# Recurrent stage of a two-layer decoder: the input added to the output projection by a product with the unit matrix, the sum copied by ScalarE

## The chip, the core and the metric

The kernel runs on one core of a Trainium2 chip. The core has five engines that each work through a queue of their own: TensorE (PE, matrix products; its results go to the accumulator memory PSUM), VectorE (DVE), ScalarE (ACT), GpSimd (POOL) and SyncE (SP, which here only starts transfers). They wait for one another through semaphores. The metric is the device time of one execution of the whole kernel in microseconds (us). Durations of single instructions are given in us too, unless marked ns. TensorE's clock has two levels, 1.2 and 2.4 GHz; the profile gives the granted clock as a share of the upper one, so that 0.50 is 1.2 GHz for a whole stretch and 1.00 is 2.4 GHz.

## The reference, cut to what matters

The whole is a decoder of two layers over x of (8, 256, 128). The change is in the second layer's recurrent ("mamba") part, four blocks in a row, each of which adds its result to its input:

```python
def _mamba(x, in_w, cw, cb, xw, dtw, dtb, A_log, Dp, ow):
    xz = x @ in_w
    u, z = jnp.split(xz, 2, axis=-1)
    ...
    u = jax.nn.silu(conv)
    dbl = u @ xw
    dt = jax.nn.softplus(dbl[..., :DT_RANK] @ dtw + dtb)
    ...
    y = _selective_scan(u, dt, A, Bm, Cm, Dp)
    y = y * jax.nn.silu(z)
    return y @ ow

def _forward(x, ...):
    for i in range(N_BLOCKS):
        h = _layer_norm(x, norm_w[i], norm_b[i])
        h = _mamba(h, in_proj_w[i], ...)
        x = x + h
    return _layer_norm(x, fn_w, fn_b)
```

The line `x = x + h` is what the change moves to other engines. The scan inside is `h = dA_t * h + dBu_t` over time, for 256 channels and 16 states each.

## The kernel before, in words

The stages of the decoder follow one another: opening (linear attention), cross attention, feed-forward, a norm, the recurrent stage (`mamba_stage`, from about 480 to 1399 us of the span), a norm, cross attention, experts, store. The change touches `mamba_stage` alone.

In this stage the tokens lie along the free axis, 2048 in all, in four quarters of 512 columns. The stage works on units that this text calls **frames**: frame f is block f // 4 and quarter f % 4, so there are 16 of them (NF). The running x of the residual lies in `xm` (the same buffer as `c.xn`, 128 channels by 2048 columns), one slice `cols(f)` per quarter, which frame f + 4 reads again.

Within a frame 16 **items** (t = 0 to 15, k = 16 f + t) go through a pipeline over four engines:

- GpSimd `times_b(k)` (L1586) makes the input of the scan, 128x1024, into one of 8 slots of `hs`, three items ahead of the scan;
- ScalarE `decay(k)` (L1769, two instructions of 512 columns) writes the decay factors into one of two pairs of PSUM banks. It may do so only when the item two before is done with them, so it runs one item ahead of VectorE and waits for VectorE's work on item k - 2;
- VectorE `scan(k)` (L1905) runs the recurrence over 1024 columns. For 11 items of 16 it multiplies the outcome by C as well (`times_c`, L1911); for t = 0, 4, 6, 10, 14 GpSimd does that (L1594);
- TensorE `sum_y` (L1663) adds up the states of four items in PSUM.

Between the items stand, at fixed values of t, the steps of the frames before and behind. On VectorE: `gate(f - 1, 1)` at t = 1, `step_size(f + 1)` at t = 8 (L1888), `gate(f, 0)` at t = 9 (L1894), `residual(f - 1)` at t = 11 (L1899) and `scaled_x(f + 2)` at t = 14 (L1880). On ScalarE: `silus(f + 1)` at t = 2 (L1797 to L1804, two loads of the function table and four activations, which need the projections of TensorE), `square` at t = 10, `inv_std` at t = 13, `affine` at t = 15 (L1793, it writes `hn`, the normalized input of the next frame), and four copies `kv_copy` (L1777) at t = 4, 7, 12, 14.

TensorE's order is written out by hand too. The part that matters is this: at the start of a frame `tap_projection(F, 0)` (L1630, four products of 512 columns; it waits for `hn`), `sum_y` of the last four items of the frame before, `skip`, `tap_projection(F, 1)`, `gate_projection`, `x_projection`; later in the frame `centre(G)` (L1690), `out_projection(f - 1)` (L1671), one `kv_job`, `average(G)` (L1694), another `kv_job`, `sum_y(f, 2)`. `average(G)` overwrites the PSUM bank PA that `out_projection(f - 1)` has filled, so it waits for the semaphore `resid`, which the residual raises. A product of fp32 operands is two MATMUL instructions in the trace; so `out_projection`, two products, is x4 there, and a tap projection is x8.

The residual of frame f - 1 is read again by `centre(f + 3)`, one frame and more later, and by the norm behind the stage; the transfers of the weights of blocks 2 and 3 wait for `resid` as well.

After the last frame come `gate(15, 1)`, `out_projection(15)` and `residual(15)`, and then all engines meet before the norm.

`w.prepare` and `rates` are GpSimd's and ScalarE's work on the next block's weights in frames 2, 6 and 10; these three are called prepare frames here.

Of the kernel before, what the change touches and what calls it, by code (L numbers as in the profile page):

```python
# [12 lines left out]
ALU = mybir.AluOpType  # L13
ACT = mybir.ActivationFunctionType
# [1374 lines left out]
def mamba_stage(c, g):  # L1389
# [31 lines left out]
    with Stage(c, "ma") as s:  # L1421
# [89 lines left out]
        with nc.Block() as block:  # L1511
# [109 lines left out]
            def _(pe):  # L1621
# [45 lines left out]
                def out_projection(f):  # L1667
                    b = (f // QUARTERS) % 2
                    pe.wait_ge(gated, 2 * f + 2)
                    for h in range(2):  # L1670
                        mm = pe.matmul(c.ps[:, PA, :], w_out[:, b, h, :], z[:, f % 3, h, :], start=(h == 0), stop=(h == 1))  # L1671
                    mm.then_inc(out_ps, 1)

# [81 lines left out]
            def _(act):  # L1755
# [50 lines left out]
                def x_rows(F):  # L1806
# [3 lines left out]
                    act.activation(xp[0:XB, :], c.ps[0:XB, PB, :], ACT.Copy).then_inc(xp_done, 1)  # L1810

                def magnitude(F):
                    if F >= 1:
                        act.wait_ge(dt_out0, 32 * F)
                        act.wait_ge(dt_out1, 32 * F)
                    for h, bank in ((0, PA), (1, PB)):
                        act.wait_ge(dt_ps, 2 * F + h + 1)
                        a = act.activation(dtu[:, h, :], c.ps[:, bank, :], ACT.Abs)
                    a.then_inc(abs_done, 1)
# [27 lines left out]
                for f in range(NF):  # L1847
                    F, G = f + 1, f + 2
                    for t in range(ITEMS):
# [16 lines left out]
                        if G < NF:  # L1866
                            if t == 10:
                                square(G)
                            if t == 13:
                                inv_std(G)  # L1870
                            if t == 15:
                                affine(G)
                        if t == 14 and f % QUARTERS == 1 and f // QUARTERS + 1 < NBLK:
                            rates(f // QUARTERS + 1)

            @block.vector
            def _(dve):
# [17 lines left out]

                def residual(f):
                    dve.wait_ge(out_ps, f + 1)
                    x = xm[:, cols(f)]
                    dve.tensor_tensor(x, x, c.ps[:, PA, :], ALU.add).then_inc(resid, 1)  # L1899

                def scan(k):
# [15 lines left out]
                for f in range(NF + 1):  # L1917
                    F, G = f + 1, f + 2
                    if f == NF:
                        gate(f - 1, 1)  # L1920
                        residual(f - 1)
                        break
                    for t in range(ITEMS):
# [8 lines left out]
                        if t == 9:  # L1932
                            gate(f, 0)
                        if t == 11 and f >= 1:
                            residual(f - 1)
                        if t == 14 and G < NF:
# [305 lines left out]
```

## Time and profile before

| | us |
|---|---|
| median of 3 runs | 1829.61 |
| lowest, highest | 1823.79, 1832.76 |
| the profiled execution, its own time | 1830.69 |
| span of the profiled execution, first to last instruction | 1829.0 |
| VectorE busy in the span | 1443.8 (79%) |
| TensorE busy | 1330.1 (73%) |
| GpSimd busy | 1141.3 (62%) |
| ScalarE busy | 1106.2 (60%) |
| mean granted TensorE clock | 0.851 |

The shares are means over stages with different limits. What bears on this change is the recurrent stage alone. A frame is measured below from one `scaled_x` (L1880) on VectorE to the next; fourteen of these lie in the loop, from 571.96 to 1283.60 us.

### The profile page before, as it was taken

The page shows a single profiled execution, that of the slowest core. Times are in us where ns is not written, and L with a number is a line of the kernel's source. Part 1 is how long each engine was busy: PE and PEld are TensorE (multiplying, and loading weights), DVE is VectorE, ACT ScalarE, POOL GpSimd, SP SyncE. Part 2 cuts the span into 40 slices and gives each one's busy share as a digit, 9 for nine tenths or more (in the row PEclk, how much of TensorE's full clock was granted, in tenths as well). Part 3 has the DMA queues.
Part 4 walks back from the last instruction along what each step waited for, and adds up shares of the span by engine and source line. Part 5 has one row for each costly group of instructions (what it writes and reads, how often), then busy time and mean ns, then how long its engine had stood idle before and what let it go on. Part 6 is the DMA issues. An engine that isn't in the chain of part 4 may idle for free. (4 is left out here: it accounts for less than half of the span.)

```text
span 1829.0 us, 23410 instructions
## 1 busy us (share of the span) xinstructions
PE 1330.1 (73%) x6866; PEld 650.4 (36%) x6867; DVE 1443.8 (79%) x2463; ACT 1106.2 (60%) x2434; POOL 1141.3 (62%) x742
## 2 busy tenths in 40 slices
PE   6777998966757557767557657557645798899878
PEld 4554555643222112222112222112201555565523
DVE  4664888877259999999999999999996577777634
ACT  4444887856565566665566665566643677677630
POOL 2111665640079999999999999999993244444400
PEclk9998999995678777787777878778867799999979
DMA  3000000000054443353454343444224111211000
GB/s 98 1 2 1 2 2 1 1 25 1 6 221 152 184 185 145 122 192 128 184 191 160 133 161 132 186 185 173 106 103 137 48 47 50 91 46 47 1 0 23
DMA packets 70218, 168.04 MB, mean 92 GB/s; under 512 B 20420, under 2 KB 40152, under 8 KB 56664
## 3 DMA queue, kind: packets, MB, share of 16 engines
q1 hardware_dynamic: 68680, 166.17, 24.5%
q8 instruction: 49, 0.80, 0.2%
q10 hardware_dynamic: 1168, 0.53, 0.1%
q14 instruction: 65, 0.53, 0.1%
q0 software_dynamic: 256, 0.01, 0.0%
HBM read 131.03 MB, written 35.65 MB: 91 GB/s over the span
## 5 line engine op out<-in xcount | busy, mean ns | idle before, releaser
L1586 POOL TENSOR_TENSOR ma_hs<-ma_dtuR,ma_Bt 128x1024 f32<-128x1024 f32 x256 | 597.0, 2360 | 30.4 <-PE ps L1663 23.3
L1769 ACT ACTIVATE ps<-ma_dtR,ma_A 128x512 f32<-128x512 f32 x512 | 332.6, 682 | 314.3 <-DVE ma_hs L1911 271.5
L844 POOL TENSOR_TENSOR x_pr<-x_pr,x_rec 128x512 f32<-128x512 f32 x256 | 267.7, 1046 | 293.1 <-DVE x_rec L1084 293.1
L1905 DVE TENSOR_TENSOR_SCAN ps<-ps,ma_hs 128x1024 f32<-128x1024 f32 x176 | 401.8, 2283 | 1.9 <-POOL ma_hs L1586 1.8
L1050 ACT ACTIVATE x_pr<-x_sm,x_mx 128x256 f32<-128x256 f32 x512 | 255.3, 500 | 71.6 <-DVE x_mx L1075 68.9
L1663 PE MATMUL ps<-ma_hs,ma_fold 128*32 128x512 f32 x1024 | 163.9, 770 | 163.2 <-POOL ma_hs L1594 151.0
L1911 DVE TENSOR_TENSOR ma_hs<-ps,ma_Ct 128x1024 f32<-128x1024 f32 x176 | 215.4, 1224 | 6.1
L1905 DVE TENSOR_TENSOR_SCAN ma_hs<-ps,ma_hs 128x1024 f32<-128x1024 f32 x80 | 182.5, 2281 | 31.0 <-ACT ps L1769 28.7
L1630 PE MATMUL ps<-ma_hn,ma_w_tap 128*128 128x512 f32 (+3 forms) x256 | 145.1, 721 | 79.0 <-ACT ma_hn L1793 79.0
L1594 POOL TENSOR_TENSOR ma_hs<-ma_hs,ma_Ct 128x1024 f32<-128x1024 f32 x80 | 188.5, 2356 | 13.5 <-DVE ma_hs L1905 13.5
L906 PE MATMUL ps<-ident,x_pr 128*128 128x128 f32 x1024 | 163.2, 286 | 5.8 <-DVE x_pT L984 4.6
L906 PEld LDWEIGHTS ps<-ident,x_pr 128*128 128x128 f32 x1024 | 113.9, 143 | 76.4 <-issue 50.3
L1663 PEld LDWEIGHTS ps<-ma_hs,ma_fold 128*32 128x32 f32 x1024 | 33.3, 131 | 282.6 <-issue 157.9
L1075 DVE CUSTOM_DVE_ANT_0 x_sm<-x_sm,x_neg 128x256 f32<-128x256 f32 x256 | 110.1, 466 | 26.3 <-DVE x_sm L1071 26.3
L1071 DVE TENSOR_TENSOR x_sm<-ps,x_m 128x512 f32<-128x512 f32 x128 | 86.8, 678 | 46.9 <-PE ps L896 45.9
L1630 PEld LDWEIGHTS ps<-ma_hn,ma_w_tap 128*128 128x128 f32 x256 | 58.6, 236 | 166.4 <-issue 166.4
L1075 DVE CUSTOM_DVE_ANT_0 x_sm<-ps,x_mr 128x256 f32<-128x256 f32 x256 | 97.5, 418 | 22.9 <-PE ps L896 19.9
L896 PE MATMUL ps<-x_k,x_q 64*128 64x256 f32 x512 | 74.5, 410 | 30.5 <-DVE x_sm L1071 29.8
L1050 ACT ACTIVATION_READ_ACCUMULATOR x_pr<-x_sm,x_mx 128x1 f32 x512 | 96.4, 188 | 0.0
L984 DVE COPY x_pT<-ps 128x512 f32<-128x512 f32 x128 | 86.5, 676 | 4.8 <-PE ps L906 4.5
L986 ACT ACTIVATE x_pT<-ps 128x512 f32<-128x512 f32 x128 | 74.5, 583 | 21.6 <-PE ps L906 21.2
L659 DVE TENSOR_TENSOR la_sc<-ps,la_tri 128x512 f32<-128x512 f32 x64 | 43.3, 680 | 48.2 <-PE ps L442 48.2
(307 smaller groups left out, 2222.6 us busy)
## 6 DMA issues: line engine op xcount, KB each, us to landing
ma_dtuR<-ma_dtu_d SPq DMA_DIRECT2D x32, 1024.0 KB, 6.8
ma_dtR<-ma_dt_d SPq DMA_DIRECT2D x32, 1024.0 KB, 8.9
ma_Bt<-ma_bc_d SPq DMA_DIRECT2D x16, 1024.0 KB, 4.9
ma_Ct<-ma_bc_d SPq DMA_DIRECT2D x16, 1024.0 KB, 7.4
ma_dtu_d<-ma_dtu SPq DMA_DIRECT2D x32, 256.0 KB, 2.0
ma_dt_d<-ma_dt SPq DMA_DIRECT2D x32, 256.0 KB, 2.3
keys_d<-ma_kv SPq DMA_DIRECT2D x32, 256.0 KB, 5.0
values_d<-ma_kv SPq DMA_DIRECT2D x32, 256.0 KB, 2.6
```

Of the source, the lines that this page charges most:

```text
L844: pool.tensor_tensor(pr[:, r, :, :], pr[:, r, :, :], rec[:, r, :].unsqueeze(2).broadcast_to([P, 2, L]), ALU.mult).then_inc(pr_done, 1)
L906: mm = pe.transpose(c.ps[:, 2 + n % 2, kt * L + t * P:kt * L + (t + 1) * P], pr[:, n % RP, t, kt * P:(kt + 1) * P], c.ident[:, :])
L1050: a = act.activation(pr[:, n % RP, t, :], sm[:, n % 2, t, :], ACT.Exp, bias=mx[:, n % 2, t:t + 1], scale=-1.0, accum_out=den[:, n % RP, t: ...
L1071: dve.tensor_tensor(sm[:, n % 2, :, :], bank, m[:, ds(b * 2, 2), :], ALU.mult).then_inc(s_free, 1)
L1075: a = dve.tensor_tensor_reduce(sm[:, n % 2, t, :], bank[:, t, :] if small else sm[:, n % 2, t, :], mr[:, p, :] if small else neg[:, t, :], ...
L1586: pool.tensor_tensor(hs[:, k % SLOTS, :, :], dtuR[:, unit(f, h), q, :].unsqueeze(1).broadcast_to([P, 2, CH]), rows(Bt, k), ALU.mult).then_ ...
L1594: pool.tensor_tensor(hs[:, k % SLOTS, :, :], hs[:, k % SLOTS, :, :], rows(Ct, k), ALU.mult).then_inc(c_pool, 1)
L1630: mm = pe.matmul(out, w_tap[:, b, TAPS - 1 - e, h * P:(h + 1) * P], src, start=(e == 0), stop=(e == TAPS - 1), skip_group_check=True)
L1663: mm = pe.matmul(c.ps[q * E32:(q + 1) * E32, Y[h], :], fold[:, :], hs[:, (k0 + q) % SLOTS, a, :], start=False, stop=(j % 2 == 1 and a == 1 ...
L1769: e = act.activation(c.ps[:, 2 * (k % 2) + a, :], dtR[:, unit(f, h), q, :], ACT.Exp, scale=A[:, (f // QUARTERS) % 2, h, q, no:no + 1])
L1905: dve.tensor_tensor_scan(out, pair(k), slot(k), 0.0, ALU.mult, ALU.add).then_inc(scan_done, 1)
L1911: dve.tensor_tensor(hs[:, k % SLOTS, :, :], c.ps[:, 2 * (k % 2):2 * (k % 2) + 2, :], rows(Ct, k), ALU.mult).then_inc(c_vector, 1)
```

## The change

It takes the addition of `residual` off VectorE. TensorE adds a third product to the accumulation group of `out_projection`: the unit matrix `c.ident` times the slice of `xm`, so that the bank PA holds x + h. ScalarE copies the bank to `xm` at t = 11, in front of the `kv_copy` of t = 12, and raises `resid`; the last of them stands behind ScalarE's loop.

```diff
                     for h in range(2):
-                        mm = pe.matmul(c.ps[:, PA, :], w_out[:, b, h, :], z[:, f % 3, h, :], start=(h == 0), stop=(h == 1))
-                    mm.then_inc(out_ps, 1)
+                        pe.matmul(c.ps[:, PA, :], w_out[:, b, h, :], z[:, f % 3, h, :], start=(h == 0), stop=False)
+                    pe.matmul(c.ps[:, PA, :], c.ident[:, :], xm[:, cols(f)], start=False, stop=True).then_inc(out_ps, 1)
...
+                def residual(f):
+                    act.wait_ge(out_ps, f + 1)
+                    act.activation(xm[:, cols(f)], c.ps[:, PA, :], ACT.Copy).then_inc(resid, 1)
...
+                        if t == 11 and f >= 1:
+                            residual(f - 1)
...
+                residual(NF - 1)
...
-                def residual(f):
-                    dve.wait_ge(out_ps, f + 1)
-                    x = xm[:, cols(f)]
-                    dve.tensor_tensor(x, x, c.ps[:, PA, :], ALU.add).then_inc(resid, 1)
...
-                        residual(f - 1)
...
-                        if t == 11 and f >= 1:
-                            residual(f - 1)
```

On VectorE, items 9 to 12 of frame 1 stand in this order before. L1894 is the gate, L1905 a scan, L1911 its product with C, L1899 the residual:

```order
L1894 TENSOR_TENSOR ma_z<-ps,ma_z 128x512
L1905 SCALAR_TENSOR_TENSOR ma_hs<-ps,ma_hs 128x1024
L1905 SCALAR_TENSOR_TENSOR ps<-ps,ma_hs 128x1024
L1911 TENSOR_TENSOR ma_hs<-ps,ma_Ct 128x1024
L1899 TENSOR_TENSOR xn<-xn,ps 128x512
L1905 SCALAR_TENSOR_TENSOR ps<-ps,ma_hs 128x1024
```

The same place in the changed kernel, whose lines lie three to eight further down (L1902 gate, L1908 scan, L1914 product with C):

```order
L1902 TENSOR_TENSOR ma_z<-ps,ma_z 128x512
L1908 SCALAR_TENSOR_TENSOR ma_hs<-ps,ma_hs 128x1024
L1908 SCALAR_TENSOR_TENSOR ps<-ps,ma_hs 128x1024
L1914 TENSOR_TENSOR ma_hs<-ps,ma_Ct 128x1024
L1908 SCALAR_TENSOR_TENSOR ps<-ps,ma_hs 128x1024
```

The scan of item 12 follows directly on the product of item 11.

On ScalarE, items 8 to 13 of frame 1 before (L1781 is `square`, L1769 `decay`, L1777 `kv_copy`, L1785 and L1787 `inv_std`):

```order
L1769 ACTIVATE ps<-ma_dtR,ma_A 128x512 x6
L1781 ACTIVATE ma_sq<-ps 128x512
L1769 ACTIVATE ps<-ma_dtR,ma_A 128x512 x4
L1777 ACTIVATE ma_kv<-ps 128x512
L1769 ACTIVATE ps<-ma_dtR,ma_A 128x512 x2
L1785 ACTIVATE ma_rstd<-ps,eps 128x512
```

and now:

```order
L1769 ACTIVATE ps<-ma_dtR,ma_A 128x512 x6
L1781 ACTIVATE ma_sq<-ps 128x512
L1769 ACTIVATE ps<-ma_dtR,ma_A 128x512 x2
L1814 ACTIVATE xn<-ps 128x512
L1769 ACTIVATE ps<-ma_dtR,ma_A 128x512 x2
L1777 ACTIVATE ma_kv<-ps 128x512
L1769 ACTIVATE ps<-ma_dtR,ma_A 128x512 x2
L1785 ACTIVATE ma_rstd<-ps,eps 128x512
```

The new copy (L1814) stands between the decays of items 12 and 13; everything else keeps its place. On TensorE the piece from `skip` to the second `kv_job` of a frame is now

```order
L1655 MATMUL ps<-ma_u,ma_dD 128x512
L1690 MATMUL ps<-xn,centre 128x512
L1671 MATMUL ps<-ma_z,ma_w_out 128x512 x2
L1672 MATMUL ps<-xn,ident 128x512
L1680 MATMUL ps<-cT,ma_w_kv 128x512
L1694 MATMUL ps<-ma_sq,average 128x512
L1680 MATMUL ps<-cT,ma_w_kv 128x512
```

with L1672 as the only row that was not there before.

## Rows read from the trace of the kernel before

**Rows 1.** Waits of VectorE, 560 to 1450 us: waiting <- waited for: us, times, longest.

```profile
DVE ma_hs L1905 <- ACT ps L1769: 21.0, 12, 1.9
...
DVE ma_z L1894 <- PE ps L1663: 5.3, 6, 3.4
```

**Rows 2.** Stretches: us, busy PE, PEld, DVE, ACT, POOL (instructions), PEclk, DMA share, GB/s.

```profile
737.48:792.09 54.61, 36.28 (x112) 12.19 (x112) 52.38 (x34) 33.90 (x51) 51.28 (x26) 0.78 0.43 160
...
846.69:901.81 55.12, 34.94 (x112) 11.73 (x112) 52.74 (x35) 33.87 (x51) 54.84 (x31) 0.79 0.39 143
901.81:956.17 54.36, 35.11 (x112) 11.79 (x112) 52.30 (x35) 33.90 (x51) 53.10 (x27) 0.81 0.43 168
```

**Rows 3.** VectorE in order of time: start us, us, instruction, [idle before <- releaser].

```profile
946.45 0.68 DVE L1899 TENSOR_TENSOR xn<-xn,ps 128x512 f32<-128x512 f32 x1
947.04 2.29 DVE L1905 TENSOR_TENSOR_SCAN ps<-ps,ma_hs 128x1024 f32<-128x1024 f32 x1
```

**Rows 4.** TensorE in order of time: three first tap projections and one second.

```profile
574.33 6.30 PE L1630 MATMUL ps<-ma_hn,ma_w_tap 128*128 128x512 f32 x8 [4.31 <-ACT ma_hn L1793]
...
739.87 5.46 PE L1630 MATMUL ps<-ma_hn,ma_w_tap 128*128 128x512 f32 x8 [5.24 <-ACT ma_hn L1793]
...
904.17 5.22 PE L1630 MATMUL ps<-ma_hn,ma_w_tap 128*128 128x512 f32 x8 [5.50 <-ACT ma_hn L1793]
...
912.14 3.58 PE L1630 MATMUL ps<-ma_hn,ma_w_tap 128*128 128x512 f32 x8
```

**Rows 5.** VectorE's waits in the frames of these three taps.

```profile
582.55 0.69 DVE L1894 TENSOR_TENSOR ma_z<-ps,ma_z 128x512 f32<-128x512 f32 x1 [0.81 <-PE ps L1663]
...
592.01 2.29 DVE L1905 TENSOR_TENSOR_SCAN ma_hs<-ps,ma_hs 128x1024 f32<-128x1024 f32 x1 [1.85 <-ACT ps L1769]
...
756.71 2.29 DVE L1905 TENSOR_TENSOR_SCAN ma_hs<-ps,ma_hs 128x1024 f32<-128x1024 f32 x1 [1.85 <-ACT ps L1769]
...
920.78 2.29 DVE L1905 TENSOR_TENSOR_SCAN ma_hs<-ps,ma_hs 128x1024 f32<-128x1024 f32 x1 [1.68 <-ACT ps L1769]
```

**Rows 6.** Stretches in which the granted clock rises, columns as in Rows 2.

```profile
579.00:580.00 1.00, 1.00 (x2) 0.29 (x2) 1.00 (x1) 0.62 (x2) 1.00 (x2) 0.67 0.15 4
...
743.00:744.00 1.00, 1.00 (x3) 0.36 (x2) 1.00 (x2) 0.16 (x1) 1.00 (x1) 0.75 0.00 0
...
907.00:908.00 1.00, 1.00 (x4) 0.43 (x3) 1.00 (x1) 0.27 (x1) 1.00 (x2) 0.83 0.00 0
...
1289.00:1290.00 1.00, 1.00 (x3) 0.26 (x2) 1.00 (x2) 0.10 (x2) 1.00 (x1) 0.68 0.00 0
```

**Rows 7.** ScalarE around the place of the copy, a prepare frame and a plain one.

```profile
888.78 1.29 ACT L1769 ACTIVATE ps<-ma_dtR,ma_A 128x512 f32<-128x512 f32 x2
892.20 1.30 ACT L1769 ACTIVATE ps<-ma_dtR,ma_A 128x512 f32<-128x512 f32 x2 [2.13 <-DVE ma_hs L1911]
...
943.12 1.30 ACT L1769 ACTIVATE ps<-ma_dtR,ma_A 128x512 f32<-128x512 f32 x2 [0.98 <-DVE ma_hs L1905]
946.56 1.30 ACT L1769 ACTIVATE ps<-ma_dtR,ma_A 128x512 f32<-128x512 f32 x2 [2.15 <-DVE ma_hs L1911]
947.80 0.57 ACT L1777 ACTIVATE ma_kv<-ps 128x512 f32<-128x512 f32 x1
```

**Rows 8.** TensorE in the same two places.

```profile
888.08 1.88 PE L1671 MATMUL ps<-ma_z,ma_w_out 128*128 128x512 f32 x4
889.80 1.02 PE L1680 MATMUL ps<-cT,ma_w_kv 128*128 128x512 f32 x2
...
941.06 1.02 PE L1680 MATMUL ps<-cT,ma_w_kv 128*128 128x512 f32 x2
947.18 2.08 PE L1694 MATMUL ps<-ma_sq,average 128*128 128x512 f32 x2 [5.09 <-DVE xn L1899]
```

**Rows 9.** The end of the stage, VectorE and TensorE.

```profile
1398.81 0.69 DVE L1899 TENSOR_TENSOR xn<-xn,ps 128x512 f32<-128x512 f32 x1 [2.14 <-PE ps L1671]
...
1396.82 1.96 PE L1671 MATMUL ps<-ma_z,ma_w_out 128*128 128x512 f32 x4 [0.91 <-DVE ma_z L1894]
```

More of the change, by code:

```diff
@@ L1868, in _ @@
                                 square(G)
+                        if t == 11 and f >= 1:
+                            residual(f - 1)
+                        if G < NF:
                             if t == 13:
```

## The prediction

> **What bounds the kernel now.** I read the page's shares first and then left them, since the change touches one stage only. In the recurrent stage I cut VectorE's order of time into frames, from one `scaled_x` to the next, and asked for busy time in each [rows 2]. The reader is to see that VectorE is busy 52.30 to 52.74 of 54.36 to 55.12 us in a frame, GpSimd 51.28 to 54.84 (next to nothing left in a prepare frame, 3 us in a plain one), ScalarE 33.9 and TensorE 35 to 36. So VectorE sets the pace and GpSimd is 3 us behind it. Next VectorE's waits [rows 1]: what it waits for in the stage is above all ScalarE's `decay`, 21.0 us in 12 waits, and TensorE's `sum_y` ahead of a gate, 5.3 us. The 12 waits lie at one place of the frame, ahead of the scan of item 4, some 19 us behind `scaled_x` [rows 5].
>
> Where they come from is seen in TensorE's rows [rows 4]. The chain is `scaled_x`, `affine`, first tap projection, `sum_y` and `skip`, second tap projection, gate and x projections, `silus`, then `decay`, then the scan. The second tap projection takes 3.58 us, the first 5.22, 5.46 and 6.30 us: the same work, but it starts behind an idle time of 4.3 to 5.5 us with a granted clock of 0.50 (1.2 GHz), and the clock goes to 1.00 (2.4 GHz) while it runs. From the granted clock of one microsecond each [rows 6] the rise can be placed: 0.67 over 579 to 580 puts it at 579.66, 0.75 at 743.50, 0.83 at 907.34, 0.68 over 1289 to 1290 at 1289.64. For the three frames with rows:
>
> - tap starts 574.33, rise 5.33 later, tap takes 6.30, VectorE then loses 0.81 + 1.85 = 2.66;
> - tap starts 739.87, rise 3.63 later, 5.46, loses 1.85;
> - tap starts 904.17, rise 3.17 later, 5.22, loses 1.68 [rows 4 to 6].
>
> So tap length is 3.58 plus half the time up to the rise, and VectorE's loss in the frame is the excess over 3.58, nearly to the hundredth. One more thing stands in these rows: the rises are 163.84, 163.84 and 382.30 us apart, which is 3, 3 and 7 times 54.61, although the frames between them took 54.36, 54.61 and 55.12 [rows 2]. The rises don't follow the taps. It is the frame that settles at them: 737.48 to 792.09 is 54.61 long.
>
> **The change part by part.**
>
> *VectorE.* Residual removed, 16 times. It costs 0.68 us by itself, but 947.04 - 946.45 = 0.59 from start to start [rows 3]. Fifteen lie in the loop and are on the path: 15 x 0.59 = 8.9 us. The one at the end is below. Without it a plain frame is 54.36 - 1.68 - 0.59 = 52.09 us of VectorE plus the loss at item 4.
>
> *What is late next.* The chain to item 4 starts at `scaled_x` on VectorE. If VectorE is there 0.59 earlier, the tap starts 0.59 earlier too, but its clock rises where it did, so the tap ends only half as much earlier: the loss grows by 0.3 us. In the next frame the tap would be earlier by another 0.59 + what is left, and so on, until the frame is again as long as the distance of the rises. That is at 52.09 + loss = 54.61, loss 2.52. By the three pairs above, loss is 1.68 + 0.45 for each us beyond 3.17, so 2.52 belongs to a tap that starts 5.0 us ahead of the rise. That lies inside what the trace shows, 5.33 us at 574.33 with a loss of 2.66. I therefore expect the frames to come back to 54.6 us, with everything in the frame 5.0 - 3.6 = 1.4 us earlier against the rises, once and not per frame. Of the 8.9 us nearly all is given back: earlier by 1.4 at the last first-tap; then the last such loss is larger by 2.52 - 1.85 = 0.7; then two residuals (items 11 of the last two frames, the last of which has no tap) save 1.18. Net 1.9 us at the end of the loop.
>
> A rule stands against this. The Trainium skill, page "TensorE: Matmul & The Clock Gate", section "Part 1: The HAM clock gate (the "warmup" mystery)", says that for modeling the ramp penalty is small against a kernel and advises not to fit to it; by that rule the clock would be left out and the sum would be the full 8.9 us less the tail. The same section says that the clock's activity monitor is free-running and does not reset with the kernel; the even spacing in [rows 6] agrees with that.
>
> *GpSimd.* It has nothing new. In prepare frames it sets part of the pace; the third stretch of VectorE's wait there is GpSimd's [rows 2]. VectorE may be 0.59 earlier at item 12 against a `times_b` that is behind in those three frames; bounds 0 and 0.6 us each, I take 0, since the longer wait at item 4 hands GpSimd 0.7 us there.
>
> *ScalarE.* One copy of 128x512 from PSUM, 0.57 us as `kv_copy` takes [rows 7], 15 times in the loop. ScalarE would be idle: between the decays of items 12 and 13 it waits 2.15 us for VectorE in the plain frame, 2.13 in the prepare frame. Cost nothing if `out_ps` is there. Behind the copy on its queue stands `decay` of item 13, and for that VectorE's scan 13.
>
> *TensorE.* The product with the unit matrix: two products back to back take 889.80 - 888.08 = 1.72, so 0.86 each at 2.4 GHz and twice that at 1.2 [rows 8]. In the plain frame `out_projection` ends at 941.1 to 941.2; the sum is there at 942.0, and ScalarE reaches the copy at 944.4, 2.4 us later. In the prepare frame it ends at 889.9, sum at 890.8, copy done by 891.4; `decay` of item 13 starts at 892.20. Margin 0.8 us. So 0 in both, with an upper bound under the rivals. `average`, which now waits 5.09 us for VectorE's residual [rows 8], gets its bank about 2 us sooner; its outcome is read at t = 13 by ScalarE, which is not waiting for it, so nothing is gained.
>
> *The tail.* Here all is serial [rows 9]: the product lies ahead of the copy, + 0.86, and a copy of 0.57 stands for an addition of 0.69, - 0.12. Together + 0.75 us (0.6 to 1.6, the upper end at 1.2 GHz).
>
> *Sum* against the profiled execution: 1829.0 - 1.9 + 0.75 = 1827.85 us of span. The execution's own time lies 1.7 above its span and 1.1 above the median; taken off the median of 1829.61, the change of -1.15 gives 1828.5 us.
>
> **The rivals.**
>
> *A: the clock takes nothing back.* The loss at item 4 stays 1.7 to 1.85 (the rise moves with the tap, or the idle time ahead of it is no longer long enough). Then 8.9 - 0.75 = 8.1 us are gained: 1821.5. For it: a low clock needs some cause, and VectorE's path is otherwise clean. Against it: four rises at multiples of 54.61 [rows 6], and a tap that still follows an idle time of about 5 us [rows 4].
>
> *B: ScalarE's copy comes late.* Place: the three prepare frames, where GpSimd makes `sum_y` and so `out_projection` late. It decides once the sum is there more than 0.8 us later than worked out above. If the whole group runs at 1.2 GHz, three products are later by 0.86 each, 2.6 us, and `decay` of item 13 by 1.8, three times: 5.4 us. In plain frames the same leaves 942.0 + 2.6 = 944.6, copy done 945.2 before 946.56, no loss. Time up to 1829.6 - 1.15 + 5.4 = 1833.9, slower than before. For it: moving 1.4 us against the rises does bring more of this group under the low clock. Against it: the margin, and that a late frame pays less at its tap.
>
> *C: the low clock lasts through the whole tap.* It would then take 2 x 3.58 = 7.16 and cost VectorE 3.58 in each of some 13 frames, 1.73 more than 1.85, against 0.59 saved: + 1.14 x 13 = 15 us, 1844. It decides where the rise comes more than 5.33 us behind the tap's start, longer than any in the rows, and the rises would have to leave their spacing.
>
> **How the numbers follow.** The clock gives back the saving (1828.5): 0.66. A: 0.17. B: 0.10. C: 0.07. The range takes in A and the upper end of B and leaves out C and the outer half of A's spread: 1821 to 1834, which is also about where the runs of before lie (1823.79 to 1832.76), and these show that a median of a few runs moves by some us. A measurement of this kernel can tell about 0.5%, 9.1 us, from no change. A lies at 0.44% and is over that bound in less than half of its cases: 0.07, with 0.03 from the rest 0.10 for faster. C and a little of B: 0.08 slower. Within 0.5%: 0.82.
>
> **What would show it.** Right: VectorE's busy time in a plain frame 51.7 instead of 52.3, the frame still 54.6; the first taps 6.0 to 6.1 us long, starting 5 us ahead of the rise; VectorE's waits in the stage larger by 0.6 to 0.7 us per frame, a part of them ahead of `gate(f - 1, 1)` at t = 1. A shows as taps of 5.2 to 5.5 and frames of 54.0. B as ScalarE waiting for TensorE ahead of the copy and VectorE for `decay` at item 13. C as taps of 7.16. My number falls if the frame's length is neither 54.6 nor 54.0, or if the first taps become shorter than 5.

## The result

The changed kernel takes 1823.08 us in the median of 22 runs (1819.43 to 1830.06), the kernel before 1830.70 in 22 runs beside it (1823.79 to 1833.92). The ratio is 0.9967, with a 95% interval of 0.9956 to 0.9977: 4 to 8 us less, about a third of a percent. Ten of the 22 runs of the changed kernel lie between 1825.1 and 1830.1 us, at mean granted clocks of 0.854 to 0.858, where runs of the kernel before lie too; the other twelve, the profiled execution of 1821.99 us among them, lie between 1819.4 and 1823.1, at 0.859 to 0.863. The profiled execution has a span of 1820.3 us, against 1829.0 before.

The page of the changed kernel, busy time of the engines:

```profile
span 1820.3 us, 23474 instructions
...
PE 1331.4 (73%) x6898; PEld 647.3 (36%) x6899; DVE 1435.7 (79%) x2447; ACT 1114.2 (61%) x2450; POOL 1140.7 (63%) x742
```

VectorE's 1443.8 us have become 1435.7. Whether that is where the 8.7 us of span went is another question, and by the frames it is not. These are stretches of the changed kernel as in [rows 2], a frame each, and then the whole from the first `scaled_x` in the loop to the norm behind the stage (columns: us, busy PE, PEld, DVE, ACT, POOL with instructions, PEclk, DMA share, GB/s):

```profile
736.77:791.28 54.51, 36.71 (x114) 11.96 (x114) 51.79 (x33) 34.41 (x52) 50.99 (x26) 0.81 0.44 160
1009.77:1064.31 54.54, 36.74 (x114) 11.98 (x114) 51.80 (x34) 34.53 (x53) 51.26 (x26) 0.81 0.49 176
...
572.24:1401.15 828.91, 540.44 (x1697) 177.08 (x1697) 780.36 (x481) 504.48 (x767) 782.69 (x390) 0.80 0.40 150
```

The last of these in the kernel before:

```profile
571.96:1399.81 827.85, 527.30 (x1664) 173.91 (x1665) 789.19 (x497) 495.99 (x751) 782.85 (x390) 0.79 0.40 150
```

VectorE is busy 0.6 us less in each frame (51.79 against 52.38 in [rows 2]), and the frame is nearly as long as it was, 54.51 against 54.61. Only the first three frames of the loop are shorter by more than 0.1 us (54.85, 55.30 and 54.39 against 55.43, 55.51 and 54.58). Over the whole stretch VectorE has 8.8 us less to do and the stretch is 1.1 us longer. The recurrent stage gained nothing in this pair of executions.

The first tap projections of the changed kernel, to be read beside [rows 4]:

```profile
793.64 6.02 PE L1630 MATMUL ps<-ma_hn,ma_w_tap 128*128 128x512 f32 x8 [4.59 <-ACT ma_hn L1793]
...
848.20 6.05 PE L1630 MATMUL ps<-ma_hn,ma_w_tap 128*128 128x512 f32 x8 [4.56 <-ACT ma_hn L1793]
```

the wait that has grown on VectorE, beside [rows 5]:

```profile
801.58 0.69 DVE L1902 TENSOR_TENSOR ma_z<-ps,ma_z 128x512 f32<-128x512 f32 x1 [0.53 <-PE ps L1663]
...
811.05 2.29 DVE L1908 TENSOR_TENSOR_SCAN ma_hs<-ps,ma_hs 128x1024 f32<-128x1024 f32 x1 [1.85 <-ACT ps L1769]
```

and the rises of the clock, beside [rows 6]:

```profile
798.00:799.00 1.00, 1.00 (x3) 0.53 (x2) 1.00 (x1) 0.94 (x2) 1.00 (x2) 0.79 0.15 4
907.00:908.00 1.00, 1.00 (x3) 0.40 (x2) 1.00 (x2) 0.67 (x2) 1.00 (x2) 0.68 0.00 0
1289.00:1290.00 1.00, 1.00 (x2) 0.34 (x1) 1.00 (x2) 0.89 (x2) 1.00 (x2) 0.53 0.00 0
```

The rises are at 798.42, 907.64 and 1289.94, that is 109.22 and 382.30 apart, 2 and 7 times 54.61, as before. The tap at 793.64 starts 4.8 us ahead of its rise (3.7 before, for the tap at 794.45), takes 6.02 us (5.47), and VectorE loses 0.53 + 1.85 = 2.38 us (1.85). What the residual had cost, VectorE now spends waiting.

So in this pair the gain lies behind the stage. There the two kernels run the same instructions. The first stretch goes from the first product of the norm to the first of the router (the products with which the expert stage starts), the second from there to the end; before and after in turn:

```profile
1399.81:1747.93 348.12, 300.26 (x1841) 192.48 (x1841) 238.59 (x836) 245.56 (x711) 136.91 (x132) 0.95 0.17 60
...
1747.93:1828.90 80.97, 65.07 (x172) 23.55 (x172) 33.79 (x34) 5.50 (x10) 2.18 (x2) 0.79 0.05 13
```

```profile
1401.15:1743.26 342.11, 293.47 (x1841) 188.14 (x1841) 239.35 (x836) 245.09 (x711) 136.74 (x132) 0.98 0.17 61
...
1743.26:1820.30 77.04, 59.72 (x172) 21.56 (x172) 33.51 (x34) 5.49 (x10) 2.19 (x2) 0.84 0.05 14
```

TensorE is busy 6.8 us less with the same 1841 instructions, at a granted clock of 0.98 instead of 0.95, and the stretch is 6.0 us shorter; then 5.3 us less with the same 172, at 0.84 instead of 0.79, and 3.9 us shorter. 9.9 us in all, less 1.1 that the recurrent stage took longer and 0.3 that the changed execution was behind at the first `scaled_x` of the loop: 8.6, the 8.7 us of span but for rounding.

Last, the new operations. In a prepare frame, beside [rows 7]:

```profile
888.80 1.29 ACT L1769 ACTIVATE ps<-ma_dtR,ma_A 128x512 f32<-128x512 f32 x2
890.88 0.60 ACT L1814 ACTIVATE xn<-ps 128x512 f32<-128x512 f32 x1 [0.79 <-PE ps L1672]
891.97 1.30 ACT L1769 ACTIVATE ps<-ma_dtR,ma_A 128x512 f32<-128x512 f32 x2 [0.48 <-DVE ma_hs L1914]
```

ScalarE reaches the copy 0.79 us too early, and 0.48 us are still left ahead of the decay of item 13. At the end of the stage, beside [rows 9]:

```profile
1395.66 3.69 PE L1671 MATMUL ps<-ma_z,ma_w_out 128*128 128x512 f32 x4 [0.91 <-DVE ma_z L1902]
1399.19 1.02 PE L1672 MATMUL ps<-xn,ident 128*128 128x512 f32 x2
```

`out_projection` runs at the lower clock here nearly to its end, 3.69 us instead of 1.96.

### The profile page after: what moved, and what is told of

Read it like the earlier page. It is cut to its first block and busy times, and to the rows that moved or that the text cites. A ratio compares the mean times of both kernels' runs of the same rounds, so it can differ in the third digit from the quotient of the medians.

```text
span 1820.3 us, 23474 instructions
## 1 busy us (share of the span) xinstructions
PE 1331.4 (73%) x6898; PEld 647.3 (36%) x6899; DVE 1435.7 (79%) x2447; ACT 1114.2 (61%) x2450; POOL 1140.7 (63%) x742
## 5 line engine op out<-in xcount | busy, mean ns | idle before, releaser
L1769 ACT ACTIVATE ps<-ma_dtR,ma_A 128x512 f32<-128x512 f32 x512 | 332.7, 682 | 294.6 <-DVE ma_hs L1914 251.7
L1908 DVE TENSOR_TENSOR_SCAN ps<-ps,ma_hs 128x1024 f32<-128x1024 f32 x176 | 401.8, 2283 | 2.1 <-POOL ma_hs L1586 2.0
L1914 DVE TENSOR_TENSOR ma_hs<-ps,ma_Ct 128x1024 f32<-128x1024 f32 x176 | 215.5, 1224 | 6.0
L1908 DVE TENSOR_TENSOR_SCAN ma_hs<-ps,ma_hs 128x1024 f32<-128x1024 f32 x80 | 182.5, 2281 | 31.3 <-ACT ps L1769 28.0
L1630 PE MATMUL ps<-ma_hn,ma_w_tap 128*128 128x512 f32 (+3 forms) x256 | 152.2, 751 | 72.8 <-ACT ma_hn L1793 72.8
L1075 DVE CUSTOM_DVE_ANT_0 x_sm<-x_sm,x_neg 128x256 f32<-128x256 f32 x256 | 110.8, 468 | 24.9 <-DVE x_sm L1071 24.9
L1075 DVE CUSTOM_DVE_ANT_0 x_sm<-ps,x_mr 128x256 f32<-128x256 f32 x256 | 97.7, 420 | 22.7 <-PE ps L896 16.9
```

The lines of the kernel that those rows point to most:

```text
L1075: a = dve.tensor_tensor_reduce(sm[:, n % 2, t, :], bank[:, t, :] if small else sm[:, n % 2, t, :], mr[:, p, :] if small else neg[:, t, :], ...
L1630: mm = pe.matmul(out, w_tap[:, b, TAPS - 1 - e, h * P:(h + 1) * P], src, start=(e == 0), stop=(e == TAPS - 1), skip_group_check=True)
L1769: e = act.activation(c.ps[:, 2 * (k % 2) + a, :], dtR[:, unit(f, h), q, :], ACT.Exp, scale=A[:, (f // QUARTERS) % 2, h, q, no:no + 1])
L1908: dve.tensor_tensor_scan(out, pair(k), slot(k), 0.0, ALU.mult, ALU.add).then_inc(scan_done, 1)
L1914: dve.tensor_tensor(hs[:, k % SLOTS, :, :], c.ps[:, 2 * (k % 2):2 * (k % 2) + 2, :], rows(Ct, k), ALU.mult).then_inc(c_vector, 1)
```

## The experiments

Two theories on the frames: **G**, VectorE's saving is given back because the first tap starts earlier against a rise of the clock that doesn't move with it; and its rival, that the loss at item 4 is ScalarE's own or has some other cause. On the gain behind the stage there were three in turn: **E** (the expert stage meets less low clock), **L** (it depends on where the norm starts against the rises), **P** (it is the one product more at the end of the stage).

### Filling products ahead of the first tap, in both kernels

```diff
                     if F < NF:
+                        if F >= 2:
+                            pe.wait_ge(lnv_done, F + 1)
+                            for _n in range(5):
+                                pe.matmul(c.ps[:, PA, :], c.ident[:, :], c.cT[:, 0:CH], start=True, stop=True)
                         tap_projection(F, 0, PA)
```

> The kernel before, with five products more on TensorE (unit matrix times a constant tile, into bank PA, results unused) between the last sum of a frame and the first tap projection, in frames 2 to 15: they fill 4.3 of the 5.2 to 5.5 us in which TensorE waits there. Theory G (the clock gives back): with the clock at its upper level the first tap takes 3.6 to 4 us, VectorE's loss at item 4 falls from 1.85 to about 0 and frames are 52.7 to 53 us; 14 frames, 20 to 26 us less, 1805 to 1811. If the loss is ScalarE's own (its two table loads and four activations, whatever the clock): taps shorter, loss unchanged, 1829 to 1831.

> The changed kernel with the same filling products. Theory G: with no low clock at the tap nothing gives the residual's 0.59 us back, so VectorE alone would allow frames of 52.1 us, 8 us less than the kernel before with the filling. GpSimd's own work is 51.25 us in a plain frame and 54.8 to 55 in a prepare frame, 52.6 on the mean of four, so it may hold the frames there: then 1 to 4 us less than the kernel before with the filling, and waits of VectorE for GpSimd. If the residual is given back for another reason: the same time as the kernel before with the filling.

Measured: 1818.39 us from before (ratio 0.9938, 0.9920 to 0.9956) and 1807.15 from the changed kernel (0.9881, 0.9860 to 0.9902). A tap, VectorE's wait at item 4 and a plain frame, of the filled kernel before:

```profile
1004.56 3.65 PE L1630 MATMUL ps<-ma_hn,ma_w_tap 128*128 128x512 f32 x8 [0.85 <-ACT ma_hn L1797]
...
1019.84 2.29 DVE L1909 TENSOR_TENSOR_SCAN ma_hs<-ps,ma_hs 128x1024 f32<-128x1024 f32 x1 [0.34 <-ACT ps L1773]
...
1002.20:1055.22 53.02, 37.98 (x122) 12.42 (x120) 52.30 (x34) 33.79 (x52) 50.45 (x25) 0.84 0.51 181
1055.22:1110.95 55.73, 38.80 (x125) 13.07 (x124) 52.70 (x35) 33.76 (x51) 55.45 (x32) 0.85 0.38 142
```

and the frames of the filled changed kernel, with the stretch from the first `scaled_x` to the norm:

```profile
1000.37:1052.79 52.42, 38.71 (x122) 12.80 (x121) 51.70 (x33) 34.33 (x53) 50.28 (x26) 0.84 0.52 183
1052.79:1108.55 55.76, 39.32 (x126) 13.28 (x125) 52.10 (x33) 34.87 (x52) 55.48 (x32) 0.85 0.36 137
...
572.63:1381.29 808.66, 571.59 (x1833) 190.57 (x1832) 779.23 (x481) 503.52 (x767) 783.32 (x390) 0.85 0.41 154
```

The tap takes 3.65 us, VectorE's loss is 0.34: it was the clock. ScalarE's table loads and activations are all still there, so the rival falls. And now the change delivers: plain frames of 52.42 against 53.02, 0.60 us, where the forecast had 0.59 for the residual. The second prepare frame and the third are 55.7 in both, with GpSimd busy 55.5 of it. Of the thirteen frames in the loop eight are 0.5 to 0.7 shorter and five are not: two prepare frames, two frames behind a prepare frame in which VectorE waits 1.04 and 1.10 us for GpSimd, and one of 54.28 us, 1.2 longer than in the filled kernel before. That one is the clock again. The filling products themselves started at the lower clock (its rise is at 894.9) and took 5.73 us, where a filling of nine instructions at the upper clock took 4.03, and VectorE waits 1.85 us for `decay` at item 4; from the filled changed kernel:

```profile
892.52 5.73 PE L1705 MATMUL ps<-cT,ident 128*128 128x512 f32 x10
898.08 3.58 PE L1630 MATMUL ps<-ma_hn,ma_w_tap 128*128 128x512 f32 x8
```

The stretch is 808.66 against 814.05, 5.4 us. I had expected 20 to 26 us from the filling alone and got 12, in part because two prepare frames got longer by 0.5 and 0.6 (55.12 before) instead of shorter. The 11.2 us between the two medians are more than either branch expected. In the profiles 5.4 of them are this stage's; the stretch from the norm to the router is 349.2 against 347.8, and the one behind it 81.0 against 75.1, although the edit touches neither.

### The same saving with the other sign

Each frame's addition done twice:

```diff
                         if t == 11 and f >= 1:
+                            dve.wait_ge(out_ps, f)
+                            dve.tensor_tensor(spare[:, :], xm[:, cols(f - 1)], c.ps[:, PA, :], ALU.add)
                             residual(f - 1)
```

> The kernel before with the residual's addition done twice in each frame, once into an unused tile: 0.59 us more for VectorE in 15 frames, the change's saving with the other sign. Theory G: the frames stay at 54.4 to 54.6 us, VectorE's loss at item 4 falls from 1.85 to about 1.3, first taps start 1.2 us nearer to the rise and take 4.9; the loop from the third scaled_x to the last stays at 711 to 713 us. If VectorE's work counts in full: frames 55.1 to 55.2, loop 718, kernel 9 us slower, 1839. What the later stages make of it I can't say, up to 6 us either way.

Measured: 1841.95 us (1.0068, 1.0053 to 1.0084), frames of 55.0 to 56.4, and a loop of 722.6 us from the third `scaled_x` to the last instead of the 711 to 713 expected (711.6 before). Theory G as I had put it is too broad: an addition is not swallowed. Two taps that follow one another:

```profile
853.83 5.11 PE L1631 MATMUL ps<-ma_hn,ma_w_tap 128*128 128x512 f32 x8 [5.58 <-ACT ma_hn L1794]
...
909.21 6.42 PE L1631 MATMUL ps<-ma_hn,ma_w_tap 128*128 128x512 f32 x8 [5.90 <-ACT ma_hn L1794]
```

With longer frames the taps slide towards the rise: the one at 853.83 starts 2.9 us ahead of it and takes 5.11. The next doesn't take 4.9 but 6.42, since its rise comes 5.6 us behind its start, 58.0 us behind the rise before it and not 54.6. In no frame of this run does the rise come less than 2.88 us behind the tap's start (the shortest tap takes 5.08). What keeps it from coming closer is not shown. In this direction the whole 0.6 us is paid, and some more: 11.0 us in the loop, where 13 additions are 7.7.

### Filling products in the expert stage

```diff
+                for _n in range(6):
+                    pe.matmul(c.ps[:, 3, :], c.ident[:, :], c.cT[:, 0:CH], start=True, stop=True)
                 pe.wait_ge(picked, 1)
...
+                for _n in range(2):
+                    pe.matmul(c.ps[:, 3, :], c.ident[:, :], c.cT[:, 0:CH], start=True, stop=True)
                 pe.wait_ge(consts, 4)
```

> The kernel before with eight filling products on TensorE in the expert stage (six ahead of the transposes of the choice, two ahead of the bias products, into an unused bank). They keep TensorE busy in 5 and 1.7 of the 7.8 and 1.4 us in which it waits there. Theory E (of the 7.6 us between the medians, some 6 are the expert stage meeting the low clock less long, because the stage now starts elsewhere against the clock's changes): expert rounds run at 2.45 us from the first or second on, the kernel before is some 6 to 8 us faster and its runs lie closer together. If the 6 us come from elsewhere, no more than 1 to 2 us.

> The changed kernel with the same filling products in the expert stage. Theory E: about 1820, the slower group of its runs (1825 to 1830) gone, and the distance to the kernel before with the filling is only what the recurrent stage gained, 0 to 3 us. If the change is worth 7 us by itself: 7 us less than the kernel before with the filling.

Measured: 1826.08 us (0.9976, 0.9965 to 0.9986) and 1818.93 us (0.9945, 0.9931 to 0.9959). Each got 4 us faster, and the distance between the medians stayed, 7.2 us. As the account of the whole, theory E falls. For a part it holds: behind the router the profiled executions now take 72.4 and 74.2 us (81.0 and 77.0 without the filling), so the 3.9 us in favour of the changed kernel there are gone, and its six runs lie within 3.9 us (1816.8 to 1820.7), where the 22 without the filling spread over 10.6. What took the place of the 3.9 us in these two executions is the recurrent stage, 826.4 us in the changed kernel against 828.4. (The profiled execution of the kernel before with the filling, 1822.55 us, is 3.5 under its median.) The largest piece of the distance is from the norm to the router, before and after in turn:

```profile
1399.91:1748.42 348.51, 299.72 (x1841) 191.92 (x1841) 238.71 (x836) 245.56 (x711) 137.00 (x132) 0.96 0.17 60
```

```profile
1398.61:1740.84 342.23, 293.54 (x1841) 188.13 (x1841) 239.33 (x836) 245.19 (x711) 136.98 (x132) 0.98 0.17 61
```

348.5 and 342.2, in another execution of each, with the numbers of the first pair to within half a microsecond. So for these two kernels it was met twice. Whether it belongs to the change, the next runs say.

### Starting the norm later, and the product alone

An addition of 128x1024 on VectorE behind the last residual; then the product with the unit matrix in every frame, with a copy on VectorE; then that in the last frame alone; then the changed kernel without it in the last frame.

```diff
                         residual(f - 1)
+                        dve.tensor_tensor(z[:, 2, :, :], z[:, 2, :, :], c.ps[:, PA:PB + 1, :], ALU.add)
                         break
```

> The kernel before with one addition of 128x1024 more on VectorE behind the last residual, its result unused: the norm and all that follows start some 1.15 us later and nothing else changes. Theory L (the stages from the norm to the experts take 342 instead of 348 us in the changed kernel because they start about 1.1 us later against the rises of the clock): this stretch falls from 348 to about 342 and the kernel is some 5 us FASTER for the added work, about 1825. If the 6 us come from anything else in the change: 1 us slower, about 1831, stretch still 348.

```diff
                     for h in range(2):
-                        mm = pe.matmul(c.ps[:, PA, :], w_out[:, b, h, :], z[:, f % 3, h, :], start=(h == 0), stop=(h == 1))
-                    mm.then_inc(out_ps, 1)
+                        pe.matmul(c.ps[:, PA, :], w_out[:, b, h, :], z[:, f % 3, h, :], start=(h == 0), stop=False)
+                    pe.matmul(c.ps[:, PA, :], c.ident[:, :], xm[:, cols(f)], start=False, stop=True).then_inc(out_ps, 1)
...
-                    dve.tensor_tensor(x, x, c.ps[:, PA, :], ALU.add).then_inc(resid, 1)
+                    dve.tensor_copy(x, c.ps[:, PA, :]).then_inc(resid, 1)
```

> Only TensorE's part of the change: the product with the unit matrix is in, and VectorE copies the sum where it added before. VectorE's work per frame is as before or a tenth of a microsecond less, so frames of 54.5 to 54.6 and taps of 5.2 to 5.5 as before; the end of the stage is 0.9 to 1.8 us later for the added product. By theory L this alone brings the stretch from the norm to the experts to about 342 and the kernel to about 1825. If the change's gain is VectorE's freed time: 1830 to 1832.

```diff
                     for h in range(2):
-                        mm = pe.matmul(c.ps[:, PA, :], w_out[:, b, h, :], z[:, f % 3, h, :], start=(h == 0), stop=(h == 1))
+                        mm = pe.matmul(c.ps[:, PA, :], w_out[:, b, h, :], z[:, f % 3, h, :], start=(h == 0), stop=(h == 1 and f < NF - 1))
+                    if f == NF - 1:
+                        mm = pe.matmul(c.ps[:, PA, :], c.ident[:, :], xm[:, cols(f)], start=False, stop=True)
                     mm.then_inc(out_ps, 1)
...
-                    dve.tensor_tensor(x, x, c.ps[:, PA, :], ALU.add).then_inc(resid, 1)
+                    if f == NF - 1:
+                        dve.tensor_copy(x, c.ps[:, PA, :]).then_inc(resid, 1)
+                    else:
+                        dve.tensor_tensor(x, x, c.ps[:, PA, :], ALU.add).then_inc(resid, 1)
```

> The kernel before with the product with the unit matrix in the last frame alone (VectorE copies the sum there). Theory P: what makes the stretch from the norm to the experts shorter in the changed kernel is this one product at the end of the recurrent stage, which keeps TensorE busy for 0.9 us more right ahead of the norm and moves the norm against the clock's rises without an idle time (the pad on VectorE had lengthened the idle time ahead of the norm to 2.2 us). Then: frames as before, norm 0.9 to 1.8 us later, low clock from the norm on first at 11.8 and then at 35.7 us behind its start, stretch 342 to 347 instead of 348, kernel 3 to 6 us faster, 1825 to 1827. If the gain needs the change in the frames: 1830 to 1832, stretch 348.

```diff
                     for h in range(2):
-                        pe.matmul(c.ps[:, PA, :], w_out[:, b, h, :], z[:, f % 3, h, :], start=(h == 0), stop=False)
-                    pe.matmul(c.ps[:, PA, :], c.ident[:, :], xm[:, cols(f)], start=False, stop=True).then_inc(out_ps, 1)
+                        mm = pe.matmul(c.ps[:, PA, :], w_out[:, b, h, :], z[:, f % 3, h, :], start=(h == 0), stop=(h == 1 and f == NF - 1))
+                    if f < NF - 1:
+                        mm = pe.matmul(c.ps[:, PA, :], c.ident[:, :], xm[:, cols(f)], start=False, stop=True)
+                    mm.then_inc(out_ps, 1)
...
-                residual(NF - 1)
...
                         gate(f - 1, 1)
+                        dve.wait_ge(out_ps, NF)
+                        dve.tensor_tensor(xm[:, cols(NF - 1)], xm[:, cols(NF - 1)], c.ps[:, PA, :], ALU.add).then_inc(resid, 1)
```

> The changed kernel with the last residual as before (two products, VectorE adds); the 15 residuals in the loop stay with TensorE and ScalarE. Theory P: the gain of the later stages goes, stretch 346 to 350 us, and only what the loop gained and the shorter tail remain: 1827 to 1830. If the gain is the loop's: 1820 to 1823, as the changed kernel or 1 to 2 us better.

The last two columns are of the profiled execution, which need not lie at the median:

| kernel | median us | ratio, interval | profiled execution, us | norm to router, PEclk there |
|---|---|---|---|---|
| before, addition at the end | 1835.43 | 1.0029, 1.0017 to 1.0040 | 1837.44 | 350.6, 0.94 |
| product in all frames, VectorE copies | 1825.70 | 0.9968, 0.9953 to 0.9983 | 1831.52 | 346.9, 0.96 |
| product in the last frame alone | 1828.70 | 0.9995, 0.9983 to 1.0007 | 1826.07 | 343.9, 0.97 |
| changed, last frame as before | 1828.95 | 0.9992, 0.9976 to 1.0008 | 1827.34 | 346.2, 0.97 |

The rows of the first and the last of these:

```profile
1404.14:1754.72 350.58, 302.64 (x1841) 192.62 (x1841) 238.96 (x836) 245.54 (x711) 136.99 (x132) 0.94 0.17 59
```

```profile
1402.19:1748.38 346.19, 298.36 (x1840) 191.54 (x1840) 238.82 (x836) 245.23 (x711) 136.77 (x132) 0.97 0.17 60
```

The first kernel fits neither branch of its expectation: the norm started 1.1 to 1.2 us later within the stage, and the median rose by 5.3 us, more than four times the 1.2 us of work added. Its profile places 1.2 us in the recurrent stage and 2.5 between norm and router; the profiled execution was also 3.2 us behind before the loop began, ahead of the edit. Theory L in its plain form, that a later norm makes the stretch shorter, is not borne out, but TensorE's row, the first products of the norm, shows that it was no clean shift. Ahead of them TensorE now idles 2.16 us instead of 1.04, and they take 5.37 us instead of 3.67, in part at the lower clock:

```profile
1404.14 5.37 PE L185 MATMUL ps<-xn,centre 128*128 128x512 f32 x8 [2.16 <-PEq L1511]
```

Of the other three, the product in all frames without any relief for VectorE gives 0.32% by itself, as much as the whole change. These are six runs from 1820.6 to 1831.5, so the median is a rough one, and the profiled execution is the slowest of them, so where that gain lies is not shown. Taking away only its last instance from the changed kernel takes the gain away (1828.95 against 1823.08; the two intervals, 0.9976 to 1.0008 and 0.9956 to 0.9977, just touch), as theory P expected. But the last instance alone, put into the kernel before, shortens the stretch in its profile (343.9) and not the median (0.9995).

Two kernels whose first purpose was another settle that the product is neither needed nor enough. The kernel before with the addition done twice has no such product, and its stretch is as short as the changed kernel's; the changed kernel with the fillings ahead of the taps and in the expert stage has it, and its stretch is as long as that of the kernel before. In this order:

```profile
1414.36:1756.50 342.14, 295.14 (x1841) 188.65 (x1841) 239.84 (x836) 245.33 (x711) 136.99 (x132) 0.98 0.17 61
```

```profile
1382.44:1730.56 348.12, 301.37 (x1840) 192.87 (x1840) 239.95 (x836) 245.57 (x711) 136.45 (x132) 0.96 0.17 60
```

So theory P falls too. What the short stretches have in common lies at their start. These are the first 60 us from the norm's first product, in the kernel before, the changed one, the one with the addition done twice, the changed one with the last frame as before, and the changed one with two fillings:

```profile
1399.81:1459.81 60.00, 43.79 (x158) 25.62 (x160) 28.36 (x83) 35.74 (x81) 9.36 (x9) 0.77 0.40 132
1401.15:1461.15 60.00, 42.62 (x189) 24.45 (x190) 31.76 (x95) 39.25 (x91) 11.43 (x11) 0.89 0.40 132
1414.36:1474.36 60.00, 42.55 (x188) 24.25 (x188) 31.48 (x93) 39.27 (x91) 11.46 (x11) 0.89 0.40 132
1402.19:1462.19 60.00, 43.57 (x160) 25.42 (x162) 28.59 (x84) 35.95 (x81) 9.39 (x10) 0.80 0.40 132
1382.44:1442.44 60.00, 43.78 (x162) 25.53 (x164) 28.80 (x84) 36.15 (x82) 9.59 (x10) 0.80 0.40 132
```

With a granted clock of 0.89 TensorE gets through 189 instructions in 60 us, at 0.77 through 158. One VectorE instruction of the cross attention (L1075) starts 60.9 us behind the norm's start in the kernel before, at 1460.69, and the same one 56.7 us behind it in the changed kernel, at 1457.87: 4.2 of the 6.0 us have arisen by then. Of all the profiled kernels but the two filled at three places, five have 0.89 in these 60 us and a stretch of 342.1 to 346.9 us, seven have 0.74 to 0.80 and one of 346.2 to 350.6.

These are single profiled executions, but three pairs of them run the same program up to the router, and within each pair the stretch agrees to 0.4 us (348.1 and 348.5, 342.1 and 342.2, 347.8 and 348.1).

What is shown: the stretch behind the stage takes 342 to 351 us with the same instructions, the shorter the higher the mean granted clock in it, 0.98 to 0.94; most of the difference between the changed kernel and the one before arises in its first 60 us; and edits in the recurrent stage alone move it either way. What about the end of that stage decides it, where the frames stand against the rises, the length of the last idle times, or both together, is not settled.

### How far filling carries

> The changed kernel with both sets of filling products, ahead of the first taps and in the expert stage. The two gains should add: 1807 less some 4 us, 1800 to 1805. If they overlap: 1806 to 1808.

> The changed kernel with filling products at three places: ahead of the first taps, in the expert stage, and four behind the averages of the norm after the recurrent stage, where TensorE waits 7 to 7.5 us for VectorE. With less low clock behind the norm (30.7 us in the kernel with two fillings) the stretch to the experts falls from 348 to 336 to 342: 1794 to 1800. If that clock isn't what the stretch depends on: 1805 to 1806.

> The kernel before with the same fillings at three places as the changed kernel at 1801.7 us. Filled, the clock has the least say in the time, so the pair gives what the change is worth by VectorE's freed time. Theory G: frames of 53.02 against 52.42 us in plain frames, GpSimd holds the prepare frames in both, the recurrent stage 5 to 6 us longer than in the changed kernel, and the whole 1806 to 1811. If the later stages' share (6 us and more in the kernels without filling) belongs to the change itself and not to the clock: 1813 to 1817.

The third place is behind the averages of the norm after the stage:

```diff
+                if add_to is not None:
+                    pe.wait_ge(lnv_done, base + 4)
+                    for _n in range(4):
+                        pe.matmul(c.ps[:, 4, :], c.ident[:, :], c.cT[:, 0:CH], start=True, stop=True)
```

Two places on the changed kernel: 1805.95 us (0.9869, 0.9854 to 0.9885), nearly all of it the first place's (1807.15 alone), so the two gains do not add. Three places: 1801.66 us (0.9843, 0.9821 to 0.9866), the fastest kernel of this study, 28.6 us under the kernel before, but not the 1794 to 1800 expected. The stretch from the norm to the router is 345.6 in it, not the 336 to 342 I had hoped for. Three places on the kernel before: 1807.64 (0.9882, 0.9866 to 0.9899). So with less of the lower clock the change is worth 6.0 us between the medians (7 by the two ratios, each against the kernel before beside it), and its stage shows 5.1, 808.54 against 813.60:

```profile
573.60:1382.14 808.54, 571.22 (x1834) 190.74 (x1832) 779.26 (x481) 503.42 (x767) 782.91 (x390) 0.85 0.42 154
```

```profile
570.50:1384.10 813.60, 565.49 (x1801) 187.22 (x1800) 788.73 (x497) 493.31 (x751) 782.87 (x390) 0.83 0.41 153
```

## Why the prediction was right, and where it was not

The forecast was 1828.5 us, 1.15 us less than before, and no change that counts; measured were 1823.1, 7.6 us less, and -0.33%. The time lies in the range and it is no change that counts, and the mechanism in the frames is the forecast one. But that the time lies in the range is in part luck: the range reached down to 1821 for rival A, which did not occur, and what filled that part of it was a gain behind the stage that the forecast did not have. By its steps:

- **VectorE's saving, 0.59 us per frame, given back by the clock: right**, in mechanism and nearly in size. Forecast were frames of 54.6, taps of 6.0 to 6.1 us, 5.0 us ahead of the rise, a loss of 2.52, partly ahead of `gate(f - 1, 1)`. Measured, from the fourth frame of the loop on: 54.3 to 54.6 (55.1 for prepare frames), 5.8 to 6.05 us, 4.3 to 4.8 us ahead, 2.15 to 2.4, the gate's share 0.3 to 0.55. The filled kernels show that it is the clock: with it up at the tap, the 0.6 us per frame appear.
- **The loop: right.** From the first `scaled_x` of the loop to the last it is 1.1 us shorter (710.5 against 711.6), forecast were 1.4.
- **ScalarE's copy: right.** The sum was there at 890.88 in the prepare frame (forecast 890.8), with 0.48 us left ahead of item 13. Rival B did not occur; nor did C.
- **GpSimd: right for this kernel, short of the whole.** It doesn't show where the clock holds the frame. The forecast cites [rows 2] for VectorE's wait on GpSimd in a prepare frame, but those rows show no waits; the trace has them, 0.62 us at 861.22 and 1.14 at 865.92. The same rows show GpSimd busy 53.10 of 54.36 us in the frame behind a prepare frame, which the "3 us in a plain one" passes over. With the tap's clock filled up, GpSimd holds four of the thirteen frames of the loop and one is lost to the clock, so that the stage gained 5.1 to 5.4 us, not the 8.1 of rival A.
- **The tail: mis-sized.** Forecast + 0.75 us (to 1.6). From the last `scaled_x` to the norm the terms of the forecast were - 1.18 for two residuals, + 0.7 for the last loss and + 0.75 for the tail, + 0.3 together; measured are 116.2 before and 118.4 after, + 2.2. `out_projection` alone is 1.7 longer, at the lower clock: the frames' shift against the rises shows at their end. The range of this term took 1.2 GHz for the added product only, and not for the two products ahead of it; the added one ran at 2.4 (1.02 us for its two instructions), the two ahead at 1.2.
- **What follows the stage: left out, and this is the step that failed.** The term for it was 0. The sum took everything behind the last residual as unchanged, since its instructions are. It got 6.0 and 3.9 us shorter, 9.9 against a forecast change of 1.15 in all. The same reasoning that I had used inside the loop, that the clock's changes don't move with the kernel, says that everything behind a moved point meets another clock. I used it for fourteen frames and not for the 430 us behind them.

The median comes near rival A's 1821.5, but A isn't what happened: A needed frames of 54.0, and they are 54.5.

The Trainium skill, page "TensorE: Matmul & The Clock Gate", section "Part 1: The HAM clock gate (the "warmup" mystery)", says that for modeling the ramp penalty is under 1% of a typical kernel's span, and advises against fitting a specific count of cold products. In this case it is more: filling at three places took 1.2% off each kernel (1830.2 to 1807.6 us and 1823.1 to 1801.7). For a change of a third of a percent leaving the clock out would have misled, since here it decided both where the saving went and where the gain came from.

## What to carry to other kernels

Before counting a saving on the bounding engine, look at how far apart the rises of the clock are. If the lower clock covers the start of a TensorE burst on the path and its rise doesn't move with the burst, time saved elsewhere can come back as slower products. Try covering the idle time ahead of such a burst with products whose result nobody uses; that was worth 12 us in the kernel before and 16 in the changed one, where the change by itself was worth 4 to 8. And take a gain of some tenths of a percent apart by stretches before crediting it: here it lay in stages that the edit never touched, and the kernel with its addition done twice, which has nothing of the edit, showed the same short stretch behind the norm.

## What was not expected of the hardware

- The same 1841 instructions took TensorE between 293.5 and 302.6 us, and their stretch 342.1 to 350.6 us, at mean granted clocks of 0.98 to 0.94.
- Some 1.2 us of work added to VectorE at the end of a stage cost 5.3 us of the whole (1835.43 against 1830.17). One product of 0.86 us added to TensorE in each frame, with VectorE copying where it had added, gained 4.5 (1825.70, a rough median of six runs).
- The response is one-sided: 0.6 us taken from a plain frame of 54.4 to 54.6 changed it by 0.1 or less from the fourth frame of the loop on; 0.6 us added made frames of 55.0 to 56.4.
